# First stage of a two-layer attention kernel: order of a copy, places of two loads, banks of the first turned tiles and of the last products

## The chip, the cores and the metric

The kernel runs on one core of one Trainium2 chip. The time is that of one execution on the device, in microseconds, the median of several runs. The core has five engines with a program each: TensorE (PE), ScalarE (ACT), VectorE (DVE), GpSimd (POOL) and SyncE (SP). Each works through its program in order; they meet at semaphores. SP issues all DMAs of this kernel. TensorE writes to PSUM, eight banks of 128 x 512 float32, which ACT and DVE read and POOL does not.

## The reference

Two attention layers follow each other on x and a context y, both 32 x 128 x 1024.

```
# layer 0, for each batch
q = Wq0 y + bq0;  k = Wk0 y + bk0;  v = Wv0 x + bv0      # 8 heads of 16 channels
att = softmax(q k^T / sqrt(128))                          # over channels, inside a head
o = Wo0 (att v) + bo0 + x
h = (o - mean(o)) / sqrt(var(o) + eps) * gn_w + gn_b      # mean, var over the whole batch
# layer 1, 32 heads, 8 key heads, W' = W + 2 A B
out = h + softmax((h Wq')(y Wk')^T / sqrt(32)) (y Wv') Wo'   # hidden and y as (32, 128, 1024)
```

## The kernel before

All matrix products of weight are made from two rounded parts (hi and lo, type fp32r): hi by hi, hi by lo and lo by hi, so three matmuls stand for one.

**First stage**, the loop `for b in range(B)` with B = 32, in each engine's program. For batch b:

- PE: `gram_products(b)`, eight products of turned y with itself, hi half (the gram) and mixed half (hi by lo), into bank 3; then the 24 key and value products `kv_products` (bank 2) in pieces, with the small products of layer 0 between them: `turn_gram` (the mixed half transposed), `t1_product`, `score_product`, `turn_y(b + 1)` (banks 0 and 1), `n1_product`, `mix_product`; `turn_k(b - 1)`, `prep_product` of a weight unit, and last `mixed_x(b)`, six products of x_hi and x_lo with the combined 128 x 128 matrix, into banks 4 and 5. `mean_product(b - 1)` and `var_product(b - 1)` make the normalization's sums over partitions.
- ACT: `split_x(b)` rounds x to `x_hi`, 128 x 1024; `begin_gram(b)` copies the mixed half to `gram_mixed`; `prep_round` rounds a q unit; `round_yT`, `softmax0` (the exponential), `write_h(b - 1)`, `evacuate_n1`, `round_mix`, `evacuate_kv`, `evacuate_kT`, `sum_y`.
- DVE: `partition_stats(b - 1)`, `begin_gram`, `finish_gram`, `deviation`, `evacuate_t1`, `norm_factors` (variance plus eps), `softmax0_begin`, `norm_scale` (which waits for POOL's power), `rest_yT`, `softmax0_end` (which gives `att`), `rest_yT`, `split_mix`, `rest_kT`, `prep_merge` (weight plus LoRA product).
- POOL: `x_lo = x_in - x_hi`, `prep_rest` of a q unit, `power(b - 1)` (variance to the power -0.5).
- SP: `load_y(b + 2)`, `load_x(b + 1)`, `finish_unit` (for an o unit: writes the merged tile back and loads the next raw tile in four DMAs), `write_h(b - 1)`, `write_kv(b - 1)` (one write of values, six of keys).

Units are tiles of layer 1's weights merged beside the batches: q units are rounded on ACT and finished on POOL in batches up to 16, o units in the later ones.

**The last batch** also turns the first tiles of h (`turn_h(0)` to `turn_h(3)`, four transposes each, then `round_hT` on ACT and `split_hT` on DVE). `turn_bank(i)` says in which bank a tile is turned, `turn_freed[i]` how many splits must be over. After it comes one loop over slots w on every engine; slot w holds a piece of the q projection on PE (`project_first` for w < 8) and, at fixed slots, what belongs to batch 31: its mean and variance products and `write_h`.

**The end** of the loop are 16 pairs of batches, 16 slots each. `project_o(pair, m, part)` makes product m of 7 in two halves of six matmuls, in bank `out_bank(pair, m)`; three banks, 0 to 2, serve all seven. `add_out(pair, which)`, eleven on DVE, add the products to the blocks of h, and semaphore `o` counts them. Banks 4 to 7 belong to the scores and their second pass, `bank(5 + n % 3)`, `bank(6 + n % 2)` and `bank(4 + n % 2)`.

Of the kernel before, what the change touches and what calls it, by code (L numbers as in the profile page):

```python
# [17 lines left out]
def xattn_two_layers(nc, x, ctx_4096, Wq0, bq0, Wk0, bk0, Wv0, bv0, Wo0, bo0, gn_w, gn_b,  # L18
                     Wq, Aq, Bq, Wk, Ak, Bk, Wv, Av, Bv, Wo, Ao, Bo, out):
    B, E, L = x.shape  # L20
# [9 lines left out]
    GQ = P // HD  # L30
# [3 lines left out]
    HALVES = B * NQ  # L34
    GB = 4
    NG = B // GB
    PAIRS = B // 2
# [8 lines left out]
    with ExitStack() as ctx:  # L46
# [156 lines left out]
        def bank(i):  # L203
            return banks[i // 2][:, i % 2 * BANK:(i % 2 + 1) * BANK]
# [159 lines left out]
        turn_at |= {4 * NC * (g - 1) + 4 * i + 2: 8 * g + i for g in range(2, NG) for i in range(8)}  # L364

        def turn_bank(i):
            return 3 if i < 4 else 2 + i % 2 if i < 8 else 2

        turn_freed = {}
        last_in = {}  # L370
# [23 lines left out]
            return bank(4 + n % 2)  # L394


        def out_bank(pair, m):
            return bank(2 if m in (0, 4) else (m in (2, 5)) ^ (pair % 2))


# [75 lines left out]
        def tensor_program(pe):  # L476
# [134 lines left out]
            def turn_h(i):  # L611
                b, half = divmod(i, 2)
                if turn_freed[i]:
                    pe.wait_ge(S["hT_lo"], turn_freed[i])
                elif turn_bank(i) == 3:
                    pe.wait_ge(S["gram_m"], B)
                    pe.wait_ge(S["gram_h"], B)
                else:
                    pe.wait_ge(S["kv"], B)
                pe.wait_ge(S[f"h_in{b % 2}"], DMA * (b // 2 + 1))  # L620
                for c in range(GROUP):
                    m = pe.transpose(bank(turn_bank(i))[:, c * P:(c + 1) * P],  # L622
                                     h_in[b % 2][:, (GROUP * half + c) * P:(GROUP * half + c + 1) * P], ident[:])
                m.then_inc(S["hT_mm"], 1)
# [32 lines left out]
            def project_o(pair, m, part):  # L657

                done = READS * pair
                if part == 0:  # L660
                    pe.wait_ge(S["op_lo"], PRODUCTS * pair + m + 1)
                    if pair == 0:
                        pe.wait_ge(S["wo_lo"], 2 * (m + 1))

                    if m == 0:
                        if pair:
                            pe.wait_ge(S["o"], done - 4)
                        else:
                            pe.wait_ge(S["hT_lo"], 2 * B)
                    elif m == 1:  # L670
                        if pair:
                            pe.wait_ge(S["o"], done - 1)
                        else:
                            pe.wait_ge(S["q_lo"], NC * NG - 1)
                    elif m == 2:
                        if pair:
                            pe.wait_ge(S["o"], done)
                        else:
                            pe.wait_ge(S["q_lo"], NC * NG)
                    elif m == 3:  # L680
                        pe.wait_ge(S["o"], done + 2)
                    elif m < 6:
                        pe.wait_ge(S["o"], done + 3)
                    else:
                        pe.wait_ge(S["o"], done + 6)
                for c in (2 * part, 2 * part + 1):
                    for of, w in ((0, 0), (0, 1), (1, 0)):
                        mm = pe.matmul(out_bank(pair, m), op[m][:, of, c, :], wo[m][w][:, c, :],  # L688
                                       start=c == 0 and of == 0 and w == 0, stop=c == GROUP - 1 and of == 1)
                if part == 1:  # L690
                    mm.then_inc(S["o_mm"], 1)
# [111 lines left out]
            for w in range(END):  # L803
# [11 lines left out]
                        project_o(pair, *PRODUCT_SLOTS[i])  # L815
                if w >= 4 and w in turn_at:
                    turn_h(turn_at[w])
                if w == 0:
                    mean_product(B - 1)
                if w == 1:  # L820
                    var_product(B - 1)
                if w in context_at:
                    context(context_at[w], w)
# [6 lines left out]
        def scalar_program(act):  # L830
# [171 lines left out]
            sum_y(0)  # L1002
            for b in range(B):
                last = b == B - 1
                split_x(b)
                if b:
                    begin_gram(b)
                if b and units_of(b - 1) and units_of(b - 1)[-1] < FIRST_O:
                    prep_round(units_of(b - 1)[-1])
                round_yT(b + 1, 0)  # L1010
# [24 lines left out]
            for w in range(END + 1):  # L1035
# [6 lines left out]
                    keep_product(pair)  # L1042
                if w - 1 in turn_at and turn_at[w - 1] < 8:
                    round_hT(turn_at[w - 1])
                if w == 3:
                    write_h(B - 1)
                if w in WO_PARTS:
                    out_hi(WO_PARTS[w])
# [5 lines left out]
        def vector_program(dve):  # L1054
# [343 lines left out]
            for w in range(END + 1):  # L1398
                if w in score_at:
                    maxima(score_at[w])  # L1400
                if w - 1 in turn_at:
                    split_hT(turn_at[w - 1])
                if w == 1:
                    deviation(B - 1)
                if w == 2:
                    norm_factors(B - 1)
                if w == 3:
                    norm_scale(B - 1)
                if w == 6:
                    split_q(0)  # L1410
# [129 lines left out]
        def sync_program(sp):  # L1540
# [216 lines left out]
            for b in range(B):  # L1757
                load_y(b + 2)
                load_x(b + 1)
                if b == B - 3:  # L1760

                    sp.wait_ge(S["prep_mm"], FIRST_O)
                    load_h(0)
                    load_h(1)
                if b and units_of(b - 1):
                    finish_unit(units_of(b - 1)[-1])
                if b:
                    write_h(b - 1)
                if b == B - 1:
                    load_h(2)  # L1770
                    load_h(3)
                if b:
                    write_kv(b - 1)
                for n in units_of(b)[:-1]:
                    finish_unit(n)
            write_kv(B - 1)
# [100 lines left out]
```

## Time and profile before

| | us |
|---|---|
| median of 3 runs | 1389.95 |
| lowest, highest | 1384.63, 1390.52 |
| profiled execution | 1391.53 |
| its span | 1389.7 |
| PE busy | 1339.7 (96%) |
| DVE busy | 928.3 (67%) |
| ACT busy | 824.0 (59%) |
| POOL busy | 160.1 (12%) |

The first stage fills the span up to about 412 us, the slots of the q projection and the scores up to about 880, the pairs the rest. Times in the trace count from the start of the span; the profiled execution is 1.8 us longer than its span. In the timeline a row gives start and length in us, engine, line, operation, and in brackets the idle time of the engine before it with what ended it. Neighbouring matmuls overlap, so their length is more than their pitch. Lines are those of the kernel before.

### The profile page before, as it was taken

How to read it: one execution, taken by the hardware profiler on the slowest of the kernel's cores; microseconds unless marked ns; L12 is line 12 of the kernel's file. 1: busy time of each engine (PE TensorE's matmuls, PEld its weight loads, DVE VectorE, ACT ScalarE, POOL GpSimd, SP SyncE). 2: the span in 40 equal slices, each digit the busy share in tenths (PEclk: the TensorE clock that was granted, in tenths of full speed). 3: DMA queues.
4: the chain of work that ended last, by engine and by line, in shares of the span. 5: the costliest groups of instructions: out<-in, count | busy, mean ns of one | idle time of the engine just before them, and what ended most of it. 6: DMA issues, size and time to landing. Idle time of an engine off the chain costs nothing.

```text
span 1389.7 us, 24051 instructions
## 1 busy us (share of the span) xinstructions
PE 1339.7 (96%) x7135; PEld 1052.9 (76%) x7135; DVE 928.3 (67%) x2075; ACT 824.0 (59%) x2924; POOL 160.1 (12%) x129
## 2 busy tenths in 40 slices
PE   6899999999989999999999999799999999999998
PEld 5777778887868888888888887566766767666676
DVE  5666666666654777777777775478666777666665
ACT  5556665555540677777757776376665666665440
POOL 6433333222210000000000001400000000000000
PEclk9999999999999999999999999899999999999999
DMA  7355656766656988888888888998998998977772
GB/s 200 128 197 203 203 202 205 227 222 224 222 186 214 270 253 269 265 253 257 260 255 254 256 252 255 275 281 238 251 258 239 248 256 248 249 228 232 228 212 76
DMA packets 220420, 321.42 MB, mean 231 GB/s; under 512 B 27587, under 2 KB 119333, under 8 KB 219781
## 3 DMA queue, kind: packets, MB, share of 16 engines
q1 hardware_dynamic: 220292, 319.88, 76.6%
q8 instruction: 61, 1.00, 0.3%
q14 instruction: 67, 0.54, 0.1%
HBM read 213.88 MB, written 105.91 MB: 230 GB/s over the span
## 4 chain that ended last, share of the span: by engine, by line
PE 82%; ACT 6%; DMA 4%; DVE 4%; issue 3%; SPq 2%; ACTq 0%; DVEq 0%
PE bank L651 23%; PE bank L688 21%; PE bank L547 10%; PE bank L706 7%; PE bank L738 5%; PE bank L749 5%; PE bank L622 2%; PE bank L492 2%; ACT lora_aT_kv L891 2%; DMA w_raw<-in_L_xattn_Wo 1%; DMA q_stack<-lse_dram 1%; ACT x_hi L883 1%; PE bank L572 1%; ACT kv_sb L926 1%; PE bank L577 1%
## 5 line engine op out<-in xcount | busy, mean ns | idle before, releaser
L952 ACT ACTIVATE bank<-bank,negs 128x128 f32<-128x128 f32 x1024 | 348.9, 343 | 199.1 <-DVE negs L1206 198.7
L651 PE MATMUL bank<-hT,wq 128*128 128x512 f32 x1488 | 393.4, 402 | 3.1 <-DVE hT L1166 3.1
L688 PE MATMUL bank<-wo,op 128*128 128x512 f32 x1344 | 347.4, 396 | 2.9 <-DVE h_blk L1290 2.0
L651 PEld LDWEIGHTS bank<-hT,wq 128*128 128x128 f32 x1488 | 265.3, 190 | 50.3 <-DVE hT L1166 4.1
L688 PEld LDWEIGHTS bank<-wo,op 128*128 128x128 f32 x1344 | 250.2, 189 | 55.0 <-DVE op L1261 2.4
L1201 DVE TENSOR_REDUCE maxes<-bank 128x4 f32<-128x512 f32 x256 | 175.6, 686 | 130.3 <-PE bank L706 126.4
L969 ACT ACTIVATE probT<-bank 128x512 f32<-128x512 f32 x256 | 151.4, 603 | 117.3 <-PE bank L738 114.7
L952 ACT ACTIVATION_READ_ACCUMULATOR bank<-bank,negs 128x1 f32 x1024 | 213.0, 208 | 0.0
L547 PE MATMUL bank<-wkv_hi,yT 128*128 128x512 f32 x512 | 205.5, 422 | 0.0
L706 PEld LDWEIGHTS bank<-k_stack,q_stack 96*128 96x128 f32 x1024 | 150.2, 191 | 17.0 <-DMA k_stack<-k_dram 1.0
L706 PE MATMUL bank<-k_stack,q_stack 96*128 96x128 f32 x1024 | 147.5, 267 | 0.7 <-DMA k_stack<-k_dram 0.6
L738 PE MATMUL bank<-q_stack,k_stack 98*128 98x512 f32 x256 | 109.4, 429 | 11.8 <-DMA q_stack<-lse_dram 9.2
L547 PEld LDWEIGHTS bank<-wkv_hi,yT 128*128 128x128 f32 x512 | 98.1, 192 | 14.1 <-issue 0.2
L738 PEld LDWEIGHTS bank<-q_stack,k_stack 98*128 98x128 f32 x256 | 48.1, 188 | 79.6 <-issue 48.0
L1523 POOL TENSOR_TENSOR x_lo<-x_in,x_hi 128x1024 fp32r<-128x1024 f32 x32 | 76.3, 2384 | 234.4 <-ACT x_hi L883 234.4
L547 PE MATMUL bank<-wkv_lo,yT 128*128 128x512 f32 x256 | 100.9, 394 | 0.0
L843 ACT CAST yT<-bank 128x512 fp32r<-128x512 f32 x64 | 37.1, 581 | 106.8 <-PE bank L492 106.8
L1290 DVE TENSOR_TENSOR h_blk<-bank,h_blk 128x512 f32<-128x512 f32 x80 | 53.6, 687 | 68.5 <-PE bank L688 68.5
L749 PE MATMUL bank<-probT,v_in 128*32 128x512 f32 x512 | 69.4, 615 | 0.9 <-ACT probT L969 0.8
L1261 DVE TENSOR_TENSOR op<-c_sb,op 128x512 fp32r<-128x512 f32 x96 | 67.4, 702 | 3.3
L1206 DVE TENSOR_SCALAR negs<-maxes 128x4 f32<-128x4 f32 x256 | 44.7, 175 | 27.3 <-DVE maxes L1201 0.5
L1066 DVE TENSOR_TENSOR yT<-bank,yT 128x512 fp32r<-128x512 f32 x64 | 43.8, 686 | 24.5 <-ACT yT L843 24.5
(167 smaller groups left out, 1631.4 us busy)
## 6 DMA issues: line engine op xcount, KB each, us to landing
q_stack<-q_dram SPq DMA_DIRECT2D x512, 192.0 KB, 4.5
q_dram<-q_part SPq DMA_DIRECT2D x96, 512.0 KB, 4.4
k_stack<-k_dram SPq DMA_DIRECT2D x128, 192.0 KB, 4.4
y_in<-in_ctx SPq DMA_DIRECT2D x32, 512.0 KB, 4.3
x_in<-in_x SPq DMA_DIRECT2D x32, 512.0 KB, 4.9
h_dram<-h_out SPq DMA_DIRECT2D x32, 512.0 KB, 3.9
h_in<-h_dram SPq DMA_DIRECT2D x32, 512.0 KB, 3.8
h_blk<-h_dram SPq DMA_DIRECT2D x64, 256.0 KB, 5.1
```

The lines of the kernel that those rows point to most:

```text
L547: m = pe.matmul(bank(2), yT[b % 2][:, c, part, :], w[:, c, :], start=first, stop=c == NC - 1 and part == 1)
L651: m = pe.matmul(bank(u % 2).rearrange("p (a n) -> p a n", a=2), wq[:, block, part, c, :], hT[(group + 1) % 2][:, :, of, c, :], start=c == ...
L688: mm = pe.matmul(out_bank(pair, m), op[m][:, of, c, :], wo[m][w][:, c, :], start=c == 0 and of == 0 and w == 0, stop=c == GROUP - 1 and of ...
L706: m = pe.matmul(score_bank(n)[:, j * P:(j + 1) * P], q_stack[place // GQ][SCORE_ROWS, g, j, :], k_stack[SCORE_ROWS, k % 2, g, :], start=Tr ...
L738: pe.matmul(again_bank(n), k_stack[STACK_ROWS, 2 + k % 2, g, :], again_stack(k)[STACK_ROWS, g, :, :].rearrange("p j n -> p (j n)"), start= ...
L749: m = pe.matmul(bank(3)[g * HD:(g + 1) * HD, :], v_in[:, k % 2, g, :], probT[:, (GQ * k + g) % PROBS, :], start=True, stop=True)
L952: act.activation(part, part, ACT.Exp, bias=negs[:, n % RING, j:j + 1], scale=SCORE1, accum_out=sums[:, score_column(k), g, j:j + 1]).then_ ...
L969: act.activation(probT[:, n % PROBS, :], again_bank(n), ACT.Exp, scale=SCORE1).then_inc(S["st_exp"], 1)
L1201: dve.tensor_reduce(largest, score_bank(n).rearrange("p (j t) -> p j t", j=GROUP), AX_X, ALU.max).then_inc(S["max"], 1)
L1261: dve.tensor_tensor(op_part(m, 1), tile, f32(op_part(m, 0)), ALU.subtract).then_inc(S["op_lo"], 1)
L1290: dve.tensor_tensor(block[:], *terms, ALU.add).then_inc(S["o"], 1)
L1523: pool.tensor_tensor(x_lo[:], x_in[b % 2][:], f32(x_hi[:]), ALU.subtract).then_inc(S["x_lo"], 1)
```

## The change

It has five parts.

1. ACT's `begin_gram(b)` stands ahead of `split_x(b)` for b > 0.
2. SP's `load_h(0)` and `load_h(1)`, which stood together in batch 29 behind `load_x`, stand at the end of batches 22 and 24, behind `write_kv`.
3. Turned tiles 0 to 3 of h go to banks 0 and 1 by turns instead of all to bank 3; tiles 0 and 1 wait for `yT_lo`.
4. Mean and variance products of batch 31, DVE's three steps on them and ACT's `write_h(31)` stand one slot later.
5. In the last pair, products 3 to 6 go to banks 4 to 7. They wait for the last exponentials of the second pass and of the scores instead of for additions.

```
         def turn_bank(i):
-            return 3 if i < 4 else 2 + i % 2 if i < 8 else 2
+            return i % 2 if i < 4 else 2 + i % 2 if i < 8 else 2
...
         def out_bank(pair, m):
+            if pair == PAIRS - 1 and m > 2:
+                return bank(m + 1)
             return bank(2 if m in (0, 4) else (m in (2, 5)) ^ (pair % 2))
...
                 if turn_freed[i]:
                     pe.wait_ge(S["hT_lo"], turn_freed[i])
+                elif i < 2:
+
+                    pe.wait_ge(S["yT_lo"], 2 * B)
...
+                    elif pair == PAIRS - 1:
+                        if m < 5:
+                            pe.wait_ge(S["st_exp"], HALVES * GQ)
+                        else:
+                            pe.wait_ge(S["exp"], GQ * SCORE_UNITS)
                     elif m == 3:
                         pe.wait_ge(S["o"], done + 2)
...
-                if w == 0:
+                if w == 1:
                     mean_product(B - 1)
-                if w == 1:
+                if w == 2:
                     var_product(B - 1)
...
                 last = b == B - 1
+                if b:
+                    begin_gram(b)
                 split_x(b)
-                if b:
-                    begin_gram(b)
...
-                if w == 3:
+                if w == 4:
                     write_h(B - 1)
...
                 load_x(b + 1)
-                if b == B - 3:
-
-                    sp.wait_ge(S["prep_mm"], FIRST_O)
-                    load_h(0)
-                    load_h(1)
...
                 if b:
                     write_kv(b - 1)
+                if b in (B - 10, B - 8):
+
+                    sp.wait_ge(S["prep_mm"], FIRST_O)
+                    load_h((b - B + 10) // 2)
```

The rows below are the order of instructions in the programs; those of after have its own line numbers.

On ACT, in a batch of the first stage, before: L896 scales a bias row, L883 rounds x, L871 copies the mixed gram, L854 rounds a q unit.

```order
L896 ACTIVATE s_bq<-bqk,y_sum 128x128
L854 CAST wq<-w_raw_67 128x4x4x32
L883 CAST x_hi<-x_in_55 128x1024
L871 COPY gram_mixed<-bank 128x128
L854 CAST wq<-w_raw_68 128x4x4x32
L843 CAST yT_58<-bank 128x4x128
```

The same place now:

```order
L907 ACTIVATE s_bq<-bqk,y_sum 128x128
L865 CAST wq<-w_raw_67 128x4x4x32
L882 COPY gram_mixed<-bank 128x128
L894 CAST x_hi<-x_in_55 128x1024
L865 CAST wq<-w_raw_68 128x4x4x32
L854 CAST yT_58<-bank 128x4x128
```

The copy has moved from behind the rounding of x to ahead of it; nothing else moved on ACT.

On SP, from the keys' writes of batch 28 to the raw weight tile of batch 29, before:

```order
L1615 DMA k_dram<-kT_sb_66 32x4x128 x6
L1566 DMA y_in_56<-in_ctx 128x1024
L1574 DMA x_in_55<-in_x 128x1024
L1621 DMA h_in_125<-h_dram 128x1024
L1621 DMA h_in_126<-h_dram 128x1024
L1597 DMA wo_dram<-w_raw_67 128x512
L1591 DMA w_raw_68<-in_L_xattn_Wo 32x512 x4
```

And now from the keys' writes of batch 22 to the raw tile of batch 23:

```order
L1626 DMA k_dram<-kT_sb_66 32x4x128 x6
L1632 DMA h_in_125<-h_dram 128x1024
L1577 DMA y_in_56<-in_ctx 128x1024
L1585 DMA x_in_55<-in_x 128x1024
L1608 DMA wo_dram<-w_raw_67 128x512
L1602 DMA w_raw_68<-in_L_xattn_Wo 32x512 x4
```

One load of h stands ahead of y; the second has the same neighbours two batches later, and batch 29 has none.

On PE, behind the last batch's mixing products, before: L596 turns keys, L622 a tile of h, L637 projects, L561 and L566 are the mean and the variance product of batch 31.

```order
L596 MATMUL bank<-ident,kv_sb_64 128x128 x2
L622 MATMUL bank<-ident,h_in_125 128x128 x4
L637 MATMUL bank<-hT_109,wq 128x256 x12
L561 MATMUL bank<-norm,ones_avg 128x1
L622 MATMUL bank<-ident,h_in_125 128x128 x4
L637 MATMUL bank<-hT_109,wq 128x256 x12
L566 MATMUL bank<-norm,ones_avg 128x1
```

The same place now:

```order
L599 MATMUL bank<-ident,kv_sb_64 128x128 x2
L628 MATMUL bank<-ident,h_in_125 128x128 x4
L643 MATMUL bank<-hT_109,wq 128x256 x12
L628 MATMUL bank<-ident,h_in_125 128x128 x4
L643 MATMUL bank<-hT_109,wq 128x256 x12
L564 MATMUL bank<-norm,ones_avg 128x1
L628 MATMUL bank<-ident,h_in_126 128x128 x4
```

The mean product stands behind a second turned tile and a second slot of projection.

## Rows read from the trace of the kernel before

**Rows 1.** The page's chain of waits, shares of the span by engine

```profile
PE 82%; ACT 6%; DMA 4%; DVE 4%; issue 3%; SPq 2%; ACTq 0%; DVEq 0%
```

**Rows 2.** Chain of waits in order of time: start us, us, piece

```profile
80.65 2.08 PE bank L547 x9
...
234.00 2.08 PE bank L547 x9
...
341.27 2.08 PE bank L547 x9
352.92 2.08 PE bank L547 x9
...
392.88 2.06 PE bank L547 x9
```

**Rows 3.** Timeline of batch 14, from x_hi to the next x_hi

```profile
193.56 1.03 ACT L883 CAST x_hi<-x_in 128x1024 fp32r<-128x1024 f32 x1
...
197.02 1.27 POOL L1476 TENSOR_TENSOR wq<-w_raw,wq 128x512 fp32r<-128x512 f32 x1
...
198.25 0.55 POOL L1504 TENSOR_TENSOR norm<-norm,minus_half 128x1 f32<-128x1 f32 x1
...
200.13 0.29 DVE L1144 TENSOR_SCALAR att<-att,att_stat 128x128 f32<-128x128 f32 x1
...
200.57 0.46 PE L584 MATMUL bank<-w0T,att 128*128 128x128 f32 x2
...
204.72 1.11 PE L529 MATMUL bank<-yT 128*128 128x256 f32 x8
...
205.37 1.03 ACT L883 CAST x_hi<-x_in 128x1024 fp32r<-128x1024 f32 x1
```

**Rows 4.** Timeline of batch 19, mixed gram, t1 and the softmax's end

```profile
253.81 0.30 PE L555 MATMUL bank<-ident,gram_mixed 128*128 128x128 f32 x1 [0.19 <-ACT gram_mixed L871]
...
254.22 0.29 DVE L1088 TENSOR_TENSOR gram<-bank,gram 128x128 f32<-128x128 f32 x1
...
254.78 0.47 PE L572 MATMUL bank<-w0T,gram 128*128 128x128 f32 x2
...
258.72 0.29 DVE L1144 TENSOR_SCALAR att<-att,att_stat 128x128 f32<-128x128 f32 x1
...
259.40 0.38 PE L584 MATMUL bank<-w0T,att 128*128 128x128 f32 x2
```

**Rows 5.** Timeline and chain: kT's rest (L1170), then the next batch's merge (L1077)

```profile
262.72 0.42 DVE L1170 TENSOR_TENSOR kT_sb<-bank,kT_sb 128x256 fp32r<-128x256 f32 x1 [0.87 <-ACT kT_sb L932]
...
276.22 0.04 DVE w_raw L1077
...
369.88 0.44 DVE kT_sb L1170
...
385.53 0.69 DVE L1077 SCALAR_TENSOR_TENSOR w_raw<-bank,w_raw 128x512 f32<-128x512 f32 x1 [3.53 <-DMA w_raw<-in_L_xattn_Wo]
```

**Rows 6.** Timeline of batch 31 and slot 0

```profile
406.95 0.66 PE L622 MATMUL bank<-ident,h_in 128*128 128x128 f32 x4 [0.56 <-DVE hT L1166]
...
407.17 0.27 ACT L911 COPY n<-bank 128x128 f32<-128x128 f32 x1
...
411.64 0.71 PE L607 MATMUL bank<-x_hi,mix_split 128*128 128x512 f32 x2
...
416.26 0.35 PE L561 MATMUL bank<-norm,ones_avg 128*128 128x1 f32 x2 [0.90 <-DVE norm L1104]
```

**Rows 7.** Timeline of the last pair

```profile
1361.97 9.82 PE L688 MATMUL bank<-wo,op 128*128 128x512 f32 x42
...
1368.04 0.69 DVE L1261 TENSOR_TENSOR op<-c_sb,op 128x512 fp32r<-128x512 f32 x1
...
1373.77 12.73 PE L688 MATMUL bank<-wo,op 128*128 128x512 f32 x48 [1.97 <-DVE h_blk L1290]
```

**Rows 8.** Timeline of batch 3, a wait of PE

```profile
73.50 0.50 PE L509 MATMUL bank<-lora_b_q,lora_aT_q 128*128 128x512 f32 x1 [1.08 <-DVE kT_sb L1170]
```

More of the change, by code:

```diff
@@ L1004, in scalar_program @@
                 last = b == B - 1
-                split_x(b)
                 if b:
                     begin_gram(b)
+                split_x(b)
                 if b and units_of(b - 1) and units_of(b - 1)[-1] < FIRST_O:
@@ L1402, in vector_program @@
                     split_hT(turn_at[w - 1])
-                if w == 1:
+                if w == 2:
                     deviation(B - 1)
-                if w == 2:
+                if w == 3:
                     norm_factors(B - 1)
-                if w == 3:
+                if w == 4:
                     norm_scale(B - 1)
```

## The prediction

> **What bounds the kernel now.** I read the chain of waits first: TensorE carries 82% of it [rows 1]. So an edit counts by what it does to the moments at which PE waits, and in the first stage by whatever closes the loop from one batch to the next. The first stage runs 32 batches b, one after the other on every engine. In the chain of waits the nine kv products of a batch recur: from 80.65 to 234.00 us that is 13 periods, 11.80 each; from 341.27 to 352.92 one of 11.65; from 352.92 to 392.88 three, 5.0 longer than 3 x 11.65 [rows 2]. So there are two regimes, and one accident.
>
> **The loop of batches up to 16** (these round a q unit on ACT and POOL). The timeline of batch 14 [rows 3]: ACT begins x_hi at 193.56; POOL, which waited for it, makes x_lo, then from 197.02 the rest of the q unit (1.27), and only then, at 198.25, the power. VectorE's scale waits for the power, and behind it in VectorE's program stand half of yT's rest and the two steps that finish the softmax (att ends at 200.42). PE's n1 product begins at 200.57, 0.15 later; that is the delay of a release, not slack. From there PE goes straight to the gram products of batch 15 (204.72, eight in 1.11), and ACT begins the next x_hi at 205.37. This loop is 193.56 to 205.37 = 11.81, the measured period. x_hi is on the path here although PE hardly idles.
>
> **From batch 17 on** the q unit is gone: the power no longer queues, att ends at 259.01, PE's n1 begins at 259.40 [rows 4], so 0.39 of slack. What PE waits for is the mixed gram: 0.19 idle before L555 at 253.81, and its normal pitch behind the kv product would have put it at 253.48, 0.33 earlier.
>
> **The change, part by part.**
>
> 1. *gram_mixed before x_hi, batches 2 to 16.* Before, x_hi began when ACT was free (205.37), and gram_mixed came 0.94 behind. Now ACT first waits for the gram products' end (204.72 + 1.11 = 205.83), copies (0.11 lag, then 0.16 until the next may start), and begins x_hi at about 206.10: 0.73 later. Every other step from x_hi to PE's next gram product is as it was, and the loop has no slack, so I add 0.71 to 0.73 to each period: 12.5 for 11.8. Twelve batches (5 to 16) give 8.6. Batches 3 and 4 give 0.7 and 1.0 by the same sum (in batch 4 x_hi waited for the mixing products and not for ACT, so it loses more). Batch 2 had 0.25 of slack and loses about 1.2. Batch 1 is bound on VectorE by the LoRA tiles: nothing. **+11.5.** PE gets 1.1 us of idle time per period before n1; the 0.33 that it saves at L555 goes into it. Bounds: 0 if x_hi's delay were hidden, 13.5 if batch 4's price held for all after it.
>
> 2. *The same, batches 17 to 31.* The gram copy starts 0.38 earlier, PE's L555 0.33 earlier. But t1 (L572 at 254.78) also needs VectorE's gram (L1088, 254.22 to 254.51), which stands behind the statistics; that can move up by 0.09 to 0.18, so t1 gains 0.27 at most. The path over POOL has no q unit: I sum it to 11.3 (11.81 + 0.73 - 1.23), below PE's 11.38. Fifteen periods by 0.27: **-4.1**, bounds -5 and 0. Behind this comes a limit that the trace of before shows: the o weights' raw tile is issued by SP behind the keys' six writes, y, x and the write-back, and VectorE merges it ahead of the statistics. From the end of kT's rest (262.72 + 0.42) to the merge at 276.22 are 13.1 [rows 5], mostly 11.6 to 12.1. A shorter period makes more merges late: lateness is this time less 11.4, less the lateness of the batch before (one late merge gives the next its time). By batch, 17 to 30, with 11.7 where VectorE did not wait, I get stalls that add up to 4.6 without the loads of h; before they were 2.2.
>
> 3. *Loads of h apart.* Before, two loads stood between x and the raw tile of batch 29: from kT's rest (369.88 + 0.44) to the merge are 15.2, VectorE idles 3.53 [rows 5]. Against 11.9 that is 3.3, or 1.65 a load (0.43 of SP's issue, the rest 512 KB ahead on the engines). The accident cost 4.9, of which 1.3 in slower matmuls after PE's idle time. Now each load stands at the end of batches 22 and 24, ahead of the y and x of batches 23 and 25, whose raw tiles come 1.65 later. With that the stalls add up to 7.2, against 2.2 + 4.9 before: **+0.1**, bounds -2.5 (loads hidden in the lateness already there) and +4 (each stalls by 3.3).
>
> 4. *First turned tiles in banks 0 and 1.* In batch 31 turn_h(1) waits 0.56 for the bank that ACT and VectorE are still reading, and tiles 2 and 3 wait likewise; the mixing products begin at 411.64 [rows 6]. With two banks by turns n1's copy (ACT, 407.17 to 407.44, unchanged) sets the mix product at about 407.6, half a microsecond sooner; two more tiles go without a wait, and with the steps between at their present length mix_lo is there at 409.8 and mixing begins at 410.0: -1.6. The waits added (yT_lo, long met) cost nothing. *Statistics one slot later:* PE waited 0.90 for them before L561 at 416.26 [rows 6]; a slot of 12 products plus a turned tile is 1.8, so they are ready: -1.0. What is late next is h's write, four slots behind instead of three, with tiles 8 and 9 needed only at slot 12. **-2.6**, bounds -3.5 and -1.
>
> 5. *Last pair.* Before, m3 waited for VectorE to have added m1, since it wanted m1's bank: PE idles from 1371.79 to 1373.77, and its 48 last products take 12.73 [rows 7], where the pitch of the 42 before ((9.82 - 0.39)/41 = 0.23) makes 11.2. Now m3 has bank 4, free since the last probabilities, and needs only its operand (VectorE, 1368.04 + 0.69). It begins at 1371.63, the last product ends at 1382.8 for 1386.50. The operands of m4 to m6 end by 1374.68, before their turn. The last add and its write follow at the same distance. **-3.7**, bounds -4 and -2.
>
> **Sum.** +11.5 - 4.1 + 0.1 - 2.6 - 3.7 = +1.2. The profiled execution took 1391.53 (span 1389.7), so 1392.7 for it; the median of the three runs is 1389.95, which makes **1391**. Half a per cent is 7 us, about what a measurement of this kernel can tell from no change: that is the bound of "same", 1383 to 1397.
>
> **Rivals.**
>
> *A. x_hi's delay is hidden, the change is what it looks like.* For it: in the chain of waits the ACT pieces L883 and L871 stand on the path, PE waits for the copy in both regimes, and POOL is 12% busy. Then part 1 is 0 to -3 and the sum -10 to -13: **1379**. Against it: 0.15 between att and n1 in the early batches, 0.39 in the late ones.
>
> *B. TensorE's clock falls in the early batches (slower).* New idle time of 1.1 us stands before n1 in each of 15 periods. Idle times of 1.97 were followed by slow products: the last 48 lost 1.5 [rows 7]. One of 1.08 before L509 in batch 3 was not [rows 8]. If slow products fall on the mixing and gram products behind n1, which are on the loop, a period loses 1.2 to 1.5; in half the periods that is +9 to +11: **1401**. It decides from where idle of 1.1 per 12.5 no longer holds the clock; 1.08 once is the only row near it. The Trainium skill ("TensorE: Matmul & The Clock Gate", on a second failure mode, cycling through PSUM queues) says that short idle times between groups of matmuls can make the gate swing. It speaks for this rival; the row of batch 3 does not bear it out, and one row is not a series.
>
> *C. The raw tiles set the late period.* If each load of h costs 3.3 and the shorter period is given back at the merges, parts 2 and 3 are 0 and +4: 1391 + 8 = **1398**.
>
> *D. Tail or turned tiles don't move* (m3 meets another wait): part 4 or 5 is 0, **1394**.
>
> **Chances.** Forecast 0.58, A 0.12, B 0.12, C 0.12, D 0.06. A is faster by over 0.5%; B and a third of C are slower; with a little for an underestimate of the gains in 2 and 3: faster 0.14, same 0.70, slower 0.16. The range leaves out most of A and the upper half of B: 1382 to 1400.
>
> **What would show it.** Early batches: period 12.5, x_hi 0.7 later behind kT's pieces, PE idle about 1.1 before n1 and none before the mixed gram. Late batches: near 11.4 where no merge waits, L1077 waiting in more batches by less, and no idle time of 2.7 before L561 in batch 30. Batch 31: mixing products 1.6 nearer. End: 48 products in one run with the 42. If the early period stays at 11.8, step 1 is wrong and A holds; if the products there take 0.6 instead of 0.4, B does.

## The result, and the profile after

| | before | after |
|---|---|---|
| median, us | 1389.93 (17 runs) | 1393.88 (17 runs) |
| lowest, highest | 1384.63, 1395.26 | 1390.68, 1399.22 |
| profiled execution (span) | 1391.53 (1389.7) | 1392.09 (1390.3) |

The ratio is 1.0032, 95% interval 1.0019 to 1.0044: the change costs 4.4 us, 2.6 to 6.1. That is inside the forecast range and inside what the text calls no change. The forecast sum was +1.2, so its sign was right, and 1.2 lies below the interval. What follows asks where the missing 3 us went. A difference in us behind a ratio is worked out from the ratio; it can differ by about 1 us from that of the two medians.

From here lines are those of the kernel after: the mean product is L564, the copy of the mixed gram L882, x_hi L894, the merge L1088, the last products L699.

First the page's chain of waits of after, by engine and by line:

```profile
PE 79%; DVE 5%; POOL 4%; DMA 3%; SPq 3%; ACT 3%; issue 2%; ACTq 0%; DVEq 0%; POOLq 0%
PE bank L657 24%; PE bank L699 22%; PE bank L717 7%; PE bank L550 6%; PE bank L749 5%; PE bank L760 4%; POOL x_lo L1534 3%; PE bank L610 2%; DMA w_raw<-in_L_xattn_Wo 2%; PE bank L628 2%; PE bank L532 2%; POOL wq L1487 1%; ACT x_hi L894 1%; SPq L1626 1%; PE bank L495 1%
```

PE has 79% where it had 82% [rows 1]. POOL was not in that list and now has 4%, with x_lo and the q unit; SP's issues went from 2% to 3%. The kv products (L550), which recurred in every period of the chain before [rows 2], have 6%. So a longer part of the first stage runs over other engines.

**Early batches.** Timeline of after, batch 15 (start us, length, engine, line; in brackets the idle time before):

```profile
204.05 1.05 ACT L894 CAST x_hi<-x_in 128x1024 fp32r<-128x1024 f32 x1
...
205.18 2.37 POOL L1534 TENSOR_TENSOR x_lo<-x_in,x_hi 128x1024 fp32r<-128x1024 f32 x1 [8.43 <-ACT x_hi L894]
...
207.50 1.29 POOL L1487 TENSOR_TENSOR wq<-w_raw,wq 128x512 fp32r<-128x512 f32 x1
...
208.75 0.55 POOL L1515 TENSOR_TENSOR norm<-norm,minus_half 128x1 f32<-128x1 f32 x1
...
211.06 0.46 PE L587 MATMUL bank<-w0T,att 128*128 128x128 f32 x2 [0.89 <-DVE att L1155]
...
215.20 1.12 PE L532 MATMUL bank<-yT 128*128 128x256 f32 x8
...
216.43 0.27 ACT L882 COPY gram_mixed<-bank 128x128 f32<-128x128 f32 x1 [0.48 <-PE bank L532]
...
216.59 1.05 ACT L894 CAST x_hi<-x_in 128x1024 fp32r<-128x1024 f32 x1
...
216.85 0.29 PE L558 MATMUL bank<-ident,gram_mixed 128*128 128x128 f32 x1
```

x_hi to x_hi is 12.54 us, 11.81 before [rows 3]. ACT idles 0.48 for the gram products, copies, and only then rounds x, 0.27 behind the gram products' end (215.20 + 1.12). The mixed gram's product now waits for nothing and gains nothing: PE idles 0.89 before n1 (L587) instead. From batch 5 to batch 16 every period is 12.53 to 12.57, by the starts of n1.

**Late batches.** n1 of batch 16 and of batch 31 in the timeline of after:

```profile
236.18 0.46 PE L587 MATMUL bank<-w0T,att 128*128 128x128 f32 x2 [0.90 <-DVE att L1155]
...
418.76 0.38 PE L587 MATMUL bank<-w0T,att 128*128 128x128 f32 x2
```

I call this distance the **late stretch**: fifteen periods, 182.58 us. In the trace of before it is 181.83. The shortest period up to batch 30 did fall, from 11.65 to 11.40 (the last one, into batch 31, is shorter still in every trace: 11.24 before, 10.96 after), and yet the stretch is 0.75 longer. The table of waits of VectorE, from 225 to 425 us (total us, times, longest), says why (`w_raw` is the tile of raw weight that one batch loads and the next merges); before, the same row had 7.2 us, 7 times, longest 3.5:

```profile
DVE w_raw L1088 <- DMA w_raw<-in_L_xattn_Wo: 10.0, 8, 4.2
```

The longest of them, in the timeline of batches 25 and 26:

```profile
340.26 0.53 SPq L1632 DMA_DIRECT2D h_in<-h_dram  x1
...
340.90 1.57 SPq L1577 DMA_DIRECT2D y_in<-in_ctx  x1
...
342.56 0.38 SPq L1585 DMA_DIRECT2D x_in<-in_x  x1
...
343.00 0.42 SPq L1608 DMA_DIRECT2D wo_dram<-w_raw  x1
...
343.47 2.87 SPq L1602 DMA_DIRECT2D w_raw<-in_L_xattn_Wo  x4
...
350.11 1.04 ACT L894 CAST x_hi<-x_in 128x1024 fp32r<-128x1024 f32 x1 [0.95 <-DMA x_in<-in_x]
...
351.50 0.69 DVE L1088 SCALAR_TENSOR_TENSOR w_raw<-bank,w_raw 128x512 f32<-128x512 f32 x1 [4.16 <-DMA w_raw<-in_L_xattn_Wo]
...
354.03 0.35 PE L564 MATMUL bank<-norm,ones_avg 128*128 128x1 f32 x2 [3.74 <-DVE norm L1115]
...
354.56 0.77 PE L575 MATMUL bank<-w0T,gram 128*128 128x128 f32 x2 [0.17 <-DVE gram L1099]
```

This looks like the accident of batch 29 in the kernel before (3.53 of waiting [rows 5]), now with one load of h: it is issued first, then y, x and the raw tile, whose four issues take 2.87 us; the merge is 4.16 late, PE idles 3.74, and the next product (L575) takes 0.77 where it takes 0.46 in batch 15. The clock of these 4 us, and of the early batches (stretch, length, busy us of PE, PEld, DVE, ACT, POOL, granted clock, DMA share, GB/s):

```profile
354.00:358.00 4.00, 3.80 (x16) 3.48 (x17) 1.36 (x8) 0.00 (x0) 0.55 (x1) 0.57 0.89 325
...
104.00:216.00 112.00, 104.12 (x591) 85.03 (x591) 68.50 (x224) 64.77 (x143) 37.06 (x27) 1.00 0.56 190
```

0.57 behind the long idle time is mostly the 1.2 GHz level; 1.00 in the early batches is 2.4 GHz throughout.

**Batch 31 and the end.** Timeline of after:

```profile
419.93 0.27 ACT L922 COPY n<-bank 128x128 f32<-128x128 f32 x1
...
422.75 0.71 PE L610 MATMUL bank<-x_hi,mix_split 128*128 128x512 f32 x2
...
428.45 0.28 PE L564 MATMUL bank<-norm,ones_avg 128*128 128x1 f32 x2
```

From n's copy to the mixing products are 2.82 us for 4.47, and the mean product waits for nothing, where PE had waited 0.90 [rows 6]. In the chain of waits the last 90 products, which stood in two pieces with 1.97 between them [rows 7], are one:

```profile
1366.42 20.65 PE bank L699 x90
1387.07 0.02 issue
1387.09 0.69 DVE h_blk L1301
```

From the first of the 90 to the end of the last are 20.7 us for 24.5.

The two spans differ by 0.6 only, less than the medians. Matched product by product, after is 12.0 us behind at n1 of batch 16, 12.75 at n1 of batch 31, 11.1 at the mixing products, 10.2 at 440 us of before, 9.8 from 453 to 860. Between 860 and 905 the distance falls to 4.3, in the scores, which the change does not touch: before's execution waits 2.7 longer there for loads (`q_stack<-lse_dram`, 9.2 us on its page against 6.5), and products behind that wait take 0.63 for 0.40. The traces of parts 3 to 5 together, of part 4 alone and of part 5 alone gain 2.5 to 3.6 on before's in the same place, so before's profiled execution was slow there. Without it the two traces would differ by 6.0, at the upper end of the interval of the times.

### The profile page after: what moved, and what is told of

Same layout as the page of the kernel before. It is cut to its first block, busy times and chain, and to the rows that moved or that the text cites. A ratio compares the mean times of both kernels' runs of the same rounds, so it can differ in the third digit from the quotient of the medians.

```text
span 1390.3 us, 24052 instructions
## 1 busy us (share of the span) xinstructions
PE 1334.9 (96%) x7135; PEld 1050.9 (76%) x7135; DVE 928.9 (67%) x2075; ACT 828.5 (60%) x2924; POOL 159.4 (11%) x129
## 4 chain that ended last, share of the span: by engine, by line
PE 79%; DVE 5%; POOL 4%; DMA 3%; SPq 3%; ACT 3%; issue 2%; ACTq 0%; DVEq 0%; POOLq 0%
PE bank L657 24%; PE bank L699 22%; PE bank L717 7%; PE bank L550 6%; PE bank L749 5%; PE bank L760 4%; POOL x_lo L1534 3%; PE bank L610 2%; DMA w_raw<-in_L_xattn_Wo 2%; PE bank L628 2%; PE bank L532 2%; POOL wq L1487 1%; ACT x_hi L894 1%; SPq L1626 1%; PE bank L495 1%
## 5 line engine op out<-in xcount | busy, mean ns | idle before, releaser
L699 PE MATMUL bank<-wo,op 128*128 128x512 f32 x1344 | 345.4, 394 | 0.9 <-issue 0.9
L699 PEld LDWEIGHTS bank<-wo,op 128*128 128x128 f32 x1344 | 249.0, 188 | 52.3 <-issue 2.0
L550 PE MATMUL bank<-wkv_hi,yT 128*128 128x512 f32 x512 | 202.1, 422 | 0.0
L550 PEld LDWEIGHTS bank<-wkv_hi,yT 128*128 128x128 f32 x512 | 97.9, 191 | 14.0 <-issue 0.2
L550 PE MATMUL bank<-wkv_lo,yT 128*128 128x512 f32 x256 | 100.8, 394 | 0.0
L854 ACT CAST yT<-bank 128x512 fp32r<-128x512 f32 x64 | 37.1, 582 | 85.4 <-PE bank L495 85.4
L1077 DVE TENSOR_TENSOR yT<-bank,yT 128x512 fp32r<-128x512 f32 x64 | 43.8, 686 | 24.6 <-ACT yT L854 24.6
```

The costliest lines, as they stand in the source:

```text
L550: m = pe.matmul(bank(2), yT[b % 2][:, c, part, :], w[:, c, :], start=first, stop=c == NC - 1 and part == 1)
```

## The experiments

Theory one is the prediction's sum. Its rival: the late period is set by the raw tile, so the faster period is handed back there, and a load of h costs what it happens to delay. In each run "late stretch" is as above. Ratios are to before, in the runs made beside it.

**Part 1 and 2 alone, on the kernel before.**

```
-                split_x(b)
                 if b:
                     begin_gram(b)
+                split_x(b)
```

> The kernel before with the first part alone: ACT copies the mixed gram ahead of the rounding of x. Theory (the early batches are a loop over x_hi, x_lo, the rest of the q unit and the power): the early period is 12.5 us for 11.8, the late one 11.4 where no raw tile is late; +12 us for the early batches, 0 to -3 for the late ones, together +9 to +12 over the kernel before, ratio 1.0065 to 1.0085. Rival A (x_hi's delay is hidden): early period 11.5, ratio below 1.000. Rival B (the clock falls in the early batches): kv products of 0.6 us in many early batches, ratio over 1.010.

1400.37 us against 1390.17, ratio 1.0073 (1.0054 to 1.0091): +10.1. Early period 12.55 for 11.80, as in after; shortest late period 11.41. Late stretch 185.8, longer than before by 3.9. The copy's place alone is a loss larger than the whole change's. For the late batches 0 to 3 less was expected; the profiled execution, the longest of its six, shows the opposite.

**All but parts 1 and 2**, the inverse edit, on the kernel after.

> The changed kernel with the first part undone: ACT rounds x first again; loads of h apart, turned tiles, statistics slot and last pair as changed. If the loop over x_hi is what costs, the early period is back at 11.8 us and the time is 1379 to 1384 us, ratio to the kernel before 0.992 to 0.996. If the first part costs nothing, it stays at the changed kernel's 1392 to 1394.

1383.0 us against 1390.17, ratio 0.9939 (0.9919 to 0.9960): -8.5 (-7.2 by the medians). Early period 11.80 again. Batch 24, with a load of h just ahead of its y, has a period of 16.01.

**Part 5 alone, on before.**

```
+            if pair == PAIRS - 1 and m > 2:
+                return bank(m + 1)
```

with its waits for the exponentials.

> The kernel before with the fifth part alone: the last pair's products 3 to 6 in banks 4 to 7. The 90 last products run in one piece, the last ends 3.7 us earlier than before relative to the first: -3.7 us, ratio 0.9973. Rival D (another wait takes its place): ratio 1.000.

1386.76 us, ratio 0.9975 (0.9961 to 0.9990): -3.5. The chain of waits has the 90 products in one piece:

```profile
1358.57 20.65 PE bank L695 x90
```

**POOL's power ahead of the q unit's rest, on the kernel after.** If the early loop is what I read (x_hi, x_lo, q unit, power, att, n1), taking the q unit out of it must end it.

```
+                if b:
+                    power(b - 1)
                 if b and units_of(b - 1) and units_of(b - 1)[-1] < FIRST_O:
                     prep_rest(units_of(b - 1)[-1])
-                if b:
-                    power(b - 1)
```

> The changed kernel with POOL's power ahead of the rest of the q unit, all else as changed. It takes 1.23 us out of the loop over x_hi and leaves the copy where it is. Theory: the loop is 11.3 us, below TensorE's own 11.4, so 15 early batches lose 1.1 us each against the changed kernel: -14 to -17, about 1377 us, ratio to the kernel before 0.989 to 0.993. Rival (the early period is set by the gram copy's own delay of x_hi in another way, on ACT or in x_lo): 0 to -3 against the changed kernel.

1377.01 us, ratio 0.9904 (0.9881 to 0.9928): 16.9 less than after. Timeline, the stretch shown above of after:

```profile
192.74 2.37 POOL L1534 TENSOR_TENSOR x_lo<-x_in,x_hi 128x1024 fp32r<-128x1024 f32 x1 [7.62 <-ACT x_hi L894]
...
195.07 0.54 POOL L1515 TENSOR_TENSOR norm<-norm,minus_half 128x1 f32<-128x1 f32 x1
...
195.59 1.29 POOL L1487 TENSOR_TENSOR wq<-w_raw,wq 128x512 fp32r<-128x512 f32 x1
...
196.95 0.29 DVE L1155 TENSOR_SCALAR att<-att,att_stat 128x128 f32<-128x128 f32 x1
...
197.57 0.38 PE L587 MATMUL bank<-w0T,att 128*128 128x128 f32 x2
```

The power runs directly behind x_lo, att has 0.33 of slack before n1, PE no longer waits, and the period is 11.40. With the q unit off the loop, the copy's new place is the gain that it looked like.

The late batches of this trace show something else. A raw tile makes the merge of batch 28 1.66 late, with no load of h near it, and PE idles 1.25:

```profile
364.65 0.35 PE L564 MATMUL bank<-norm,ones_avg 128*128 128x1 f32 x2 [1.25 <-DVE norm L1115]
```

In the 7.4 us behind it the granted clock is 0.77 on the average, partly at the 1.2 GHz level (same columns as above):

```profile
364.60:372.00 7.40, 7.18 (x34) 6.53 (x35) 4.24 (x16) 2.64 (x6) 1.78 (x2) 0.77 0.84 263
```

The period is 14.73, 3.3 more than the shortest, for a merge that was late by half of that. Twice more in this late stretch idle time on PE, of 1.76 and 2.56, is followed by the lower level.

**Part 3 alone, on before.**

```
-                if b == B - 3:
-                    sp.wait_ge(S["prep_mm"], FIRST_O)
-                    load_h(0)
-                    load_h(1)
...
+                if b in (B - 10, B - 8):
+                    sp.wait_ge(S["prep_mm"], FIRST_O)
+                    load_h((b - B + 10) // 2)
```

> The kernel before with the third part alone: the two loads of h at the ends of batches 22 and 24 instead of both in batch 29. The prediction's price (each load makes its raw tile 1.65 us late) gives -2 to -2.5 us, ratio 0.998, and no period over 13.5 us. The rival (a load ahead of y, x and the raw tile makes one tile late by 4 us or more wherever it stands, as the profile of the changed kernel shows in batch 25) gives one period of 16 us or more between batches 23 and 26 in place of the one of 16.5 at batch 30, and 0 us, ratio 1.000.

1385.31 us against 1388.86, ratio 0.9974 (0.9962 to 0.9987): -3.6, a little more than the first theory's time. But not by its mechanism, which allowed no period over 13.5: the period of batch 24 is 15.54 where its neighbours have 11.66, so the batch of one load stalled the loop by 3.9; that of the other, batch 26, has 12.99, where before had 12.30 one batch earlier without a load. The late stretch is 181.1 for 181.8.

**Both loads in batch 29, behind the raw tile, on before.**

```
+                if b and units_of(b - 1):
+                    finish_unit(units_of(b - 1)[-1])
                 if b == B - 3:
...
-                if b and units_of(b - 1):
-                    finish_unit(units_of(b - 1)[-1])
```

> The kernel before with its two loads of h still together in batch 29, but behind the raw tile instead of ahead of it. If the place ahead of the raw tile costs and not that they are together, the period of 16.5 us at batch 30 falls to 12 or less: -4 to -4.9 us, ratio 0.9965 to 0.997. If a megabyte in one batch costs wherever it stands, 0 to -1.5 us.

1385.67 us, ratio 0.9978 (0.9967 to 0.9990): -3.1. The period of batch 30 falls from 16.51 to 13.19, where 12 or less was expected: the merge still waits 1.8 for its tile, which was 3.5 in before. The same two transfers, in the same batch: most of what they cost depends on whether the raw tile stands behind them. The Trainium skill ("DMA: Bandwidth & Descriptors", Queues, rings and completion order) says that each DMA engine takes the descriptors of a ring in order; this pair of traces agrees with it.

**Raw tile ahead of y in the late batches, loads of h behind it, on after.**

```
-                load_y(b + 2)
-                load_x(b + 1)
...
+                if late:
+                    load_x(b + 1)
+                    finish_unit(units_of(b - 1)[-1])
+                    load_y(b + 2)
+                    if b in (B - 10, B - 8):
...
+                        load_h((b - B + 10) // 2)
```

`late` is true in the batches that load an o tile; the loads of h at the ends of batches 22 and 24 are taken out.

> The changed kernel with SP's order in batches that load an o tile altered: x, then write-back and raw tile, then y, then (batches 22 and 24) the load of h, which before stood ahead of all of them. If the raw tile's place in SP's queue is what uses up the gain of the late batches (stalls of 6 to 13 us by the profiles), late periods are 11.4 to 11.6 throughout, 15 of them 172 us for 182.6, and the time falls by 7 to 10 us against the changed kernel, ratio to the kernel before 0.996 to 0.998. If the engines of the DMA are the limit and not the place, tiles stay late and the gain is under 3 us.

1387.4 us, ratio 0.9987 (0.9973 to 1.0001): 0.0045 below after's 1.0032, which is 6.3 us, where 7 to 10 was expected. Late stretch 175.4, longest period 12.66; the waits for raw tiles fall to

```profile
DVE w_raw L1088 <- DMA w_raw<-in_L_xattn_Wo: 4.3, 5, 1.3
```

**Both edits**, the power first and SP's order just shown, on after.

> The changed kernel with both cures: POOL's power ahead of the rest of the q unit, and SP's order x, raw tile, y, h. Theory: early periods 11.43 and late ones 11.4 to 11.6, so e4_power_first's 1377 us less 7 to 10: 1367 to 1370 us, ratio to the kernel before 0.983 to 0.986. If the two share one limit, it stays at 1377.

1371.42 us, ratio 0.9882 (0.9861 to 0.9902): below both kernels, 3 us less than with the power alone (the two intervals overlap), and short of the 1367 to 1370 that I expected. Late stretch 176.1 with 5.0 us of waiting left.

**Part 2 alone, on before.**

```
+                if b > 16:
+                    begin_gram(b)
                 split_x(b)
-                if b:
+                if 0 < b <= 16:
                     begin_gram(b)
```

> The kernel before with the mixed gram copied ahead of x's rounding only in batches 17 to 31 (part 2 alone); all else is as before, the two loads of h stand together in batch 29. What the first theory (the prediction's term for part 2: 0.27 per batch, 15 batches, with raw tiles that are late a little more often) expects: shortest late period 11.40 for 11.65, the stretch from n1 of batch 16 to n1 of batch 31 178.3 for 181.8, a ratio of 0.9975. What the second (the raw tile's path, from kT's rest to the merge, does not shorten, so that each late batch hands the gain back at the next merge that waits) expects: shortest period 11.40 too, but the stretch no shorter than before, 182 to 186, as it was 185.8 in the kernel before with part 1 in all batches; a ratio of 1.000 to 1.003.

1388.48 us against 1390.92, ratio 0.9980 (0.9968 to 0.9993): -2.8, the first theory's time. The profiled execution tells the rival's: shortest period 11.42, waits for raw tiles 8.9 us in all, period of batch 30 18.36 (16.51 before), late stretch 183.0. That execution took 1392.36, the longest of its twelve, so its batch 29 may have been worse than usual. By the times, part 2 alone gains 1.0 to 4.5 us; its trace shows that the gain can be lost at one merge.

**Part 4 alone, on before.**

```
-            return 3 if i < 4 else 2 + i % 2 if i < 8 else 2
+            return i % 2 if i < 4 else 2 + i % 2 if i < 8 else 2
...
-                if w == 0:
+                if w == 1:
                     mean_product(B - 1)
```

with the wait for `yT_lo` and the later steps on batch 31 moved likewise.

> The kernel before with part 4 alone: turned tiles 0 to 3 in banks 0 and 1, statistics of batch 31 and its write one slot later. The prediction's term (1.6 from the turned tiles, 1.0 from the statistics) expects 2.6 us less, a ratio of 0.998, with n1 to the mixing products of batch 31 4.0 us for 5.63, and no idle time before the mean product. The rival (the gain is met by a later wait of the projection, for h's tiles 2 and 3 or for the write of h 31) expects mixing products as early, but the products from 20 us behind them at the same time as before, a ratio of 1.000.

1387.05 us, ratio 0.9975 (0.9963 to 0.9988): -3.5 (-1.7 to -5.1). n1 to mixing products 3.98 for 5.63, no idle time before the mean product; a given product at 453 us of before comes 2.6 nearer to n1 of batch 31, 0.4 of it also in the trace of part 5 alone. So the gain is still there behind the mixing products, and the rival is refuted.

**SP's order and part 3**, on before: as the run with the raw tile ahead, but without parts 1, 2, 4 and 5.

```
-                load_y(b + 2)
-                load_x(b + 1)
...
+                if late:
+                    load_x(b + 1)
+                    finish_unit(units_of(b - 1)[-1])
+                    load_y(b + 2)
...
```

> The kernel before with its order of copy and rounding, but SP in the batches with o units in the order x, write-back and raw tile, y, load of h (loads of h in batches 22 and 24), as in the run with raw tiles ahead. If the copy's place is worth 0.25 per batch once raw tiles come in time, the stretch from n1 of batch 16 to n1 of batch 31 is 178 to 180 here against 175.4 there, shortest period 11.65, and the ratio is 0.997 (2 to 4 us less than before, from SP's order alone). If the raw tile alone sets the late period, the stretch is the same 175.4 to 176 here, with periods below 11.65, and the ratio is 0.995.

1383.33 us, ratio 0.9943 (0.9927 to 0.9958): -7.9; theory one expected 2 to 4 less, the rival 0.995. Late stretch 177.0, between the two, shortest period 11.65, waits for raw tiles 4.0. No period up to batch 30 is below 11.65, so the copy's place is worth 0.25 in a period without a late merge; over the fifteen it is 1.6 (175.4 against 177.0, one trace each) and not 3.75. The rival is right too: the larger item was SP's order with the loads behind the raw tile. The stretch explains 4.9 of the 7.9; the rest is not explained by these traces.

**The raw tile first of all**, on the kernel with both edits (the edit as against that kernel):

```
                 if late:
-                    load_x(b + 1)
                     finish_unit(units_of(b - 1)[-1])
+                    load_x(b + 1)
                     load_y(b + 2)
```

> The kernel after with POOL's power first and, in the batches with o units, SP in the order write-back and raw tile, x, y, load of h: the raw tile one transfer further ahead than in the run before it of this kind (where x stood ahead). That one still had VectorE waiting 5.0 us in all for raw tiles, and its stretch from n1 of batch 16 to n1 of batch 31 was 176.1, where fifteen shortest periods make 171.1. If the place of x ahead of the raw tile is what is left, the stretch falls to 172 to 174, the ratio to 0.985 to 0.987. The rival: x now comes late for ACT's rounding, which waited 1.0 for it once in the kernel after; then the stretch is 176 or more and the ratio 0.988 or above.

1368.36 us (4 runs), ratio 0.9838 (0.9816 to 0.9859): the best of all kernels here, 1.6% below before. Late stretch 171.2, below the 172 to 174 expected, every period of it between 11.40 and 11.58 but the last, 10.99. Its chain of waits, by engine, and the last pieces of the kv products:

```profile
PE 94%; DVE 2%; ACT 1%; SPq 1%; DMA 1%; issue 1%; DVEq 0%; ACTq 0%
```

```profile
342.88 2.09 PE bank L550 x9
...
354.28 2.08 PE bank L550 x9
...
365.82 2.08 PE bank L550 x9
...
377.23 2.08 PE bank L550 x9
```

VectorE never waits for a raw tile and ACT never for x. The timeline of one batch shows how close it still is on SP:

```profile
314.20 0.68 DVE L1088 SCALAR_TENSOR_TENSOR w_raw<-bank,w_raw 128x512 f32<-128x512 f32 x1
...
314.35 0.32 SPq L1622 DMA_DIRECT2D v_dram<-kv_sb  x1
...
314.72 3.90 SPq L1626 DMA_DIRECT2D k_dram<-kT_sb  x6
...
318.67 0.59 SPq L1608 DMA_DIRECT2D wo_dram<-w_raw  x1
...
319.30 1.84 SPq L1602 DMA_DIRECT2D w_raw<-in_L_xattn_Wo  x4
...
321.23 0.37 SPq L1585 DMA_DIRECT2D x_in<-in_x  x1
...
321.70 0.38 SPq L1577 DMA_DIRECT2D y_in<-in_ctx  x1
```

The keys' six writes hold SP for 3.9 us, and the write-back and the raw tile follow without a gap.

The waits of VectorE for raw tiles and TensorE's mean granted clock, both from 225 to 425 us, over all traces:

| kernel | shortest period, to batch 30 | waits, us | granted clock | late stretch |
|---|---|---|---|---|
| before | 11.65 | 7.2 | 0.99 | 181.8 |
| parts 3, 4, 5 | 11.64 | 6.7 | 0.99 | 181.6 |
| part 3 alone | 11.65 | 6.6 | 0.99 | 181.1 |
| part 4 alone | 11.66 | 6.8 | 0.99 | 181.9 |
| part 5 alone | 11.65 | 6.9 | 0.99 | 181.6 |
| loads behind raw tile, on before | 11.65 | 5.6 | 1.00 | 178.5 |
| SP's order and part 3, on before | 11.65 | 4.0 | 1.00 | 177.0 |
| after | 11.40 | 10.0 | 0.99 | 182.6 |
| parts 1 and 2 | 11.41 | 10.4 | 0.97 | 185.8 |
| part 2 alone | 11.42 | 8.9 | 0.98 | 183.0 |
| after, power first | 11.40 | 10.1 | 0.97 | 185.8 |
| after, raw tile ahead | 11.40 | 4.3 | 1.00 | 175.4 |
| both edits | 11.41 | 5.0 | 1.00 | 176.1 |
| both, raw tile first | 11.40 | none | 1.00 | 171.2 |

With SP's order as it was, the traces with the shorter period wait 8.9 to 10.4 us, those with the longer one 6.6 to 7.2, apart from the one whose loads of h stand behind the raw tile. With the raw tile ahead the shorter period is kept, and the clock never falls in these batches. Each line is one execution. Those of parts 1 and 2, of part 2 and of the power first were the longest of their kernels' runs, which makes their figures high; but after's was the fourth shortest of 17 and waits 10.0, and the one with the raw tile ahead was the longest of its twelve and waits 4.3.

## Why the prediction was right, and where its sum was not

**What bounds it.** Right: two regimes, the early one a loop over ACT, POOL and VectorE without slack though PE hardly idled. The run with the power first took the q unit out of that loop and the period fell by 1.1 us, to 11.40.

**Part 1**, +11.5: after is 12.0 us behind at n1 of batch 16. The period is 12.54 for a forecast 12.5, x_hi comes 0.27 behind the gram products as summed, PE idles 0.89 to 0.91 before n1 in the batches from 3 on, but for one with 0.55 (1.1 forecast). The right size.

**Parts 2 and 3**, -4.1 and +0.1: here the sum failed, in the term for the raw tiles. The gain per period was right, 0.25 for 0.27. The late stretch of before is fifteen times 11.65 plus 7.1 of stalls, which is the 2.2 + 4.9 of the prediction. That of after is fifteen times 11.40 plus 11.6, where the prediction had 7.2. The missing 4.4, and 0.3 from 0.25 for 0.27, make -4.0 into +0.75. The step at fault is "1.65 a load": it was measured where two loads stood just ahead of the raw tile, and I charged it as a constant. Placed ahead of y and x too, the first load goes with a period 1.2 too long (12.58) and the second with one 5.7 too long (17.07): 6.9 for the 2.6 that the prediction adds for both. The other periods of after add up to 4.7 of stalls, for the 4.6 of the prediction, so that part of the sum held (in part 2 alone they are 5.0 without batch 30; in parts 1 and 2, a long execution, 8.3). Alone on before, the batch of one cost 3.9 and that of the other 1.3; behind the raw tile they cost 0.2 and 0.6 (11.60 and 11.99).

Nor is a stall of this size always a load's: batch 28 with the power first has 14.73 and batch 21 of parts 1 and 2 has 14.86, neither with a load of h near. The price of a late merge also includes the slower clock behind PE's idle time. I had this in the accident of batch 29 (1.3 of it) and left it out of the new stalls. That the raw tile's lateness is what took the gain is shown by the run that puts it ahead of y on after: the stretch falls by 7.2 and the time by 6.3.

How much of it is an effect of the parts on each other the times say only roughly: parts alone sum to +10.1 - 3.6 - 3.5 - 3.5 = -0.5, together they measure +4.4, and the intervals of the five measurements together leave some 4.5 us either way. Likewise +10.1 and -8.5 from the two runs that split off the copy make +1.6 for a measured +4.4. The times too point to parts 1 and 2, which the prediction had at +7.4 together: alone they measure +10.1, beside the other three 4.4 + 8.5 = 12.9. The direction is that of the traces: a raw tile meets less slack in a period of 11.4.

**Part 4**, -2.6: -1.65 up to the mixing products (1.6 forecast), -0.9 from them to 440 us (1.0). Alone -3.5 with an interval that holds 2.6.

**Part 5**, -3.7: 20.7 for 24.5, -3.8. Alone -3.5.

**The rivals.** A (x_hi hidden) is refuted by the period of 12.54. But its result was one line away: with the power first the same copy gives 11.40. B (the clock falls in the early batches) is refuted: the clock is 1.00 from 104 to 216 us with some 0.9 of idle time in nearly every period. The Trainium skill's rule behind it ("TensorE: Matmul & The Clock Gate", second failure mode) did not show at this size. Where the clock did fall is in the late batches, behind single idle times of 3.7 in after and of 1.25 to 2.6 with the power first. C is the one that came in part: it said parts 2 and 3 would be 0 and +4, and together they were +0.75, between it and the forecast. (Its time should read 1399: 1391 + 8.) D is refuted by the traces, in which both parts moved in full, though its 1394 is the time that was measured: the time alone could not have told it from the forecast.

**The time.** 1391 forecast, 1393.88 measured. With the terms as the traces have them, +12.0 + 0.75 - 2.9 - 3.8 makes +6.0 where the prediction had +1.2 (0.4 of the 2.9 comes between 440 and 453 us, and in the trace of part 5 alone too). Measured are +4.4, 2.6 to 6.1. The range held because a miss of 4.75 in one term is small against its width of 18, not because the sum was right.

**Open.** Why SP's issue of y took 1.57 us at 340.90 of after (and 1.66 and 1.34 in two other batches), where it takes 0.52 to 0.55 in nearly all the rest, and why in one kernel the first load of h hurts and in another the second. One profiled execution of each cannot tell a fixed phase from chance. Whether part 2 in after gains or not on the average is not known better than by its run alone.

## What to carry to other kernels

Before moving a step on an engine that seems to feed the bottleneck, look for a loop through other engines with a release gap of 0.1 to 0.2 us at its last hand-over: two loops of nearly equal length can share the path, and the one that the chain of waits does not print decides. In these runs the price of a transfer was mostly that of the deadlines queued behind it (the same two loads: a period of 16.51 with the raw tile behind them, 13.19 with it ahead): put what has a deadline every period first in the queue, and what is needed once behind it. When a period is made shorter, check each transfer that has to land once per period: here the waits for one of them rose from 7 to 10 us and took the gain, until the order on SP gave it back with more.

## What the runs showed of the hardware

Two things that I had not expected. Idle times of some 0.9 us on PE, nine of them from 104 to 216 us of after and nearly one per 12.5 us, left the granted clock at 1.00, while one of 3.7 us was followed by 4 us at 0.57 and a product of 0.77 for 0.46, and in the run with the power first one of 1.25 us by 7.4 us at 0.77. So that late merge cost 3.3 us for 1.66 of lateness. And on SP a period of 11.4 us is nearly full of issue time: six small writes of keys take 3.8 to 4.4 us, four pieces of a raw tile 1.8 to 2.9, and one issue of y, at a DMA share of 0.86 (340 to 350 us of after), took 1.57 instead of 0.54.
